# A gated cross-attention and mixture-of-experts layer: expert rows loaded two blocks at a time, and eight more zero products on TensorE at the head

## The chip, the cores and the metric

One core of a Trainium2 chip runs the whole layer in one launch. The metric is device time in microseconds; the kernel before was run three times for it, and one further execution was profiled. Engines are named as in the profile: PE is TensorE, DVE is VectorE, ACT is ScalarE, POOL is GpSimd, SP is the sync engine, which here does nothing but issue DMAs.

## The reference

4096 tokens (64 sequences of 64) of width 128, in float32:

```python
x = x + tanh(g_xattn[0]) * xattn(layernorm(x), ctx)
x = x + tanh(g_ffn[0]) * ffn(layernorm(x))

# xattn(Q, K): causal scores of K with itself, applied to Q
scores = einsum('btd,bsd->bts', K, K) * tril(ones)
return Q + einsum('bts,bsd->btd', scores, Q)

# ffn: one shared expert and the 2 best of 8 experts for each token
shared = silu(x @ shared_w1.T) @ shared_w2.T            # hidden width 512
top, idx = top_k(x @ gate_w.T, 2); gates = softmax(top)
selected = sum over the 2 experts of gate * (silu(x @ w1[e]) @ w2[e])
return shared + selected
```

## The kernel before

The tokens are 32 tiles of 128, in 8 groups of 4 tiles. The program of every engine is written out by hand, in order, with semaphores between them.

**Head (until about 74 us).** For each group PE makes the masked scores (`score`, L1099 and L1103), applies them (`apply_scores`, L1113), transposes the normalised rows n (`transpose_n`, L1120), makes logits in strips (`logit_strips`, L1128, and `logits`, L1134), and in between the shared expert's products (`shared_up`, L1164, and `shared_down`, L1177). ACT writes n tile by tile (L580), one semaphore count per tile, and `transpose_n` waits for each tile; ACT then copies the four transposed tiles out of the bank (L589) before the strips can be made. `keep_warm(times)` (L1184) issues products of a 128x128 with a 128x512 tile of zeros in bf16 into a bank that nobody reads; there are eight at the very start and five between `apply_scores(1)` and `transpose_n(0)`. DVE chooses the experts and the rows' places (`choose`, `place`); POOL then scatters the rows of n into a table in DRAM, sorted by expert, one indirect DMA per tile and choice (L516). The table's rows are 145 numbers (580 bytes): 128 of n and the routing data. The first 32 of these scatters are stage 0; SP waits for all of them before it loads any expert row.

**Expert blocks (from about 81 us).** The table is worked off in 71 blocks of 128 rows. Blocks 0 to 33 are full and come in 17 pairs: both blocks of a pair belong to one expert and lie next to each other in the table (the row of the second is that of the first plus 128). Blocks 34 to 70 stand alone. Blocks are loaded in sets of four (the first set has two): set 0 is blocks 0 and 1, set 1 is 2 to 5, set 2 is 6 to 9, set 3 is 10 to 13. `load_x(s)` on SP issues one DMA per block (L389) into a ring of 12 buffers, each with its own semaphore; ahead of each it reads the row's address into a register (L387, L388). `load_w1(i)` (L377 to L380) does the same for a 256 KB weight, one for each pair or single block, into a ring of 8.

The order on SP is: weights 0 and 1; wait for stage 0's scatters; sets 0 and 1; weights 2 and 3; set 2; weights 4 to 7; then, block by block, the next weight (its buffer is free when the up products of the pair 8 weights earlier are done, L379) and the set three further on. Weight 8 thus waits for the second up product, and set 3 stands behind it. Weight 9 also waits for DVE's second tables of addresses.

On PE `transpose_rows(s)` (L1289) waits for each block's semaphore and transposes it into one bank; DVE copies the bank to SBUF (`copy_xT`, L1007), and the next set's transposes wait for that copy. The order is set 0, the first up product (`up`, L1315), set 1, `counts`, the second up product, set 2, then for each block one up product and one down product (`down`, L1336), with set 3 ahead of the up product of block 6, set 4 ahead of that of block 10, and so on. ACT applies silu and the gate, POOL scatters each block's result to its tokens (L542), and after the last block SP and ACT load those rows back, DVE adds them, and the result is stored.

On DVE the copy of set 2 comes, in its queue, after the second tables (`tables_full`) and `region_ends`.

Of the kernel before, what the change touches and what calls it, by code (L numbers as in the profile page):

```python
# [5 lines left out]
def flamingo_gated_moe(nc, xP, ctxT, g_both, sw1T, sw2T, w1T, w2T, gateT, outP):  # L6
# [7 lines left out]
    ds = bass.ds  # L14

    P = 128
# [4 lines left out]
    E = w1T.shape[1] // H  # L21
# [4 lines left out]
    G = 4  # L26
# [23 lines left out]
    FULL = 2 * PAIRS  # L50
# [3 lines left out]
    SPARE = USED - K * TILES  # L54
    P_SHIFT = P.bit_length() - 1
    PADS = E + SPARE
    REGION = T + P
# [8 lines left out]
    SET = 4  # L66
    X_SETS = 3
# [7 lines left out]
    sets = [range(max(0, a), min(USED, a + SET)) for a in range(FULL % SET - SET, USED, SET)]  # L75
# [12 lines left out]

    def last_with(b):
        return b | 1 if b < FULL else b  # L90

    UP_BANKS, Y_BANKS = ((1, 2), (1, 2, 5, 6)), ((3, 7), (3, 7, 4))

# [13 lines left out]
    with stack:  # L107
        def sb(name, shape, dt=f32):
            return stack.enter_context(nc.sbuf_tensor(name, shape, dt))

        def sem(name):
            return stack.enter_context(nc.semaphore(name))

        x_dram = nc.dram_tensor("expert_rows", ((E + 1) * REGION, ROW), f32, kind="Internal").ap()
# [73 lines left out]
        row_at = sb("row_at", [1, USED], i32)  # L188
# [10 lines left out]
        x_ring = sb("x_ring", [P, X_RING, ROW])  # L199
# [71 lines left out]
        x_loaded = [sem(f"x_loaded{j}") for j in range(X_RING)]  # L271
# [16 lines left out]
        def at_least(eng, semaphore, value):  # L288
            if value > 0:
                eng.wait_ge(semaphore, value)  # L290
# [16 lines left out]
        def tile(g, t):  # L307
            return slice(g * GW + t * D, g * GW + (t + 1) * D)
# [28 lines left out]
        def _(sp):  # L337
# [27 lines left out]
            row_reg = [sp.alloc_register(f"sp_row{i}") for i in range(2)]  # L365
# [6 lines left out]
            def load_w1(i):  # L372
                slot_w = i % W_RING
                b = first_of(i)
                if b in (0, EARLY, FULL):
                    sp.wait_ge(tables_done, (0, EARLY, FULL).index(b) + 1)
                sp.reg_load(weight_reg[i % 2], weight_at[0:1, b:b + 1])  # L377
                at = sp.snap(weight_reg[i % 2], min_val=0, max_val=(E - 1) * H)
                at_least(sp, up_psum, last_with(first_of(i - W_RING)) + 1 if i >= W_RING else 0)  # L379
                sp.dma_start(w1_ring[:, slot_w], w1T[:, ds(at, H)]).then_inc(w1_in[slot_w], 16)  # L380

            def load_x(s):
                at_least(sp, xT_psum, s - X_SETS + 1)
                at_least(sp, gap_done, s - X_SETS + 1)
                for i, b in enumerate(sets[s]):
                    j = s % X_SETS * SET + i
                    sp.reg_load(row_reg[i % 2], row_at[0:1, b:b + 1])  # L387
                    at = sp.snap(row_reg[i % 2], min_val=0, max_val=E * REGION + (SPARE - 1) * P)  # L388
                    sp.dma_start(x_ring[:, j], x_dram[ds(at, P), :]).then_inc(x_loaded[j], 16)  # L389

            def y_complete(until):
                for j in range(Y_RING):
# [10 lines left out]
            load_w1(1)  # L403
            sp.wait_ge(x_scattered[0], 16 * STAGE_TILES[0])
            load_x(0)
            load_x(1)
            load_w1(2)
            load_w1(3)
            load_x(2)
            for i in range(4, W_RING):  # L410
                load_w1(i)
# [143 lines left out]
        def _(act):  # L555
# [151 lines left out]
            def silu(b):  # L707
                act.wait_ge(up_psum, b + 1)
                at_least(act, y_psum, last_with(b - H_SLOTS) + 1 if b >= H_SLOTS else 0)
                act.activation(hT[:, b % H_SLOTS], ps_up(b)[:, :], ACT.Silu).then_inc(hT_done, 1)  # L710
# [379 lines left out]
        def _(pe):  # L1090
# [16 lines left out]
            def apply_scores(g):  # L1107
                pe.wait_ge(scores_done, g + 1)
                at_least(pe, x1_done, g)
                for t in range(G):  # L1110
                    pe.wait_ge(q_done, G * g + t + 1)
                    cols = slice(t * P, (t + 1) * P)
                    last = pe.matmul(ps_q[:, cols], masked(g)[:, cols], q[:, g % 2, cols], start=True, stop=True)  # L1113
                last.then_inc(attn_psum, 1)

            def transpose_n(g):
                at_least(pe, strips_done, g)
                for t in range(G):
                    pe.wait_ge(n_done, G * g + t + 1)
                    last = pe.transpose(ps_n[:, t * P:(t + 1) * P], n[:, g * G + t, 0:D], ident[:, :])  # L1120
                last.then_inc(nT_psum, 1)

            def logit_strips(g):
                if g == 0:
                    pe.wait_ge(gT_in, 16)
                pe.wait_ge(nT_done, g + 1)
                for t in range(G):
                    last = pe.matmul(ps_strips[t * STRIP:(t + 1) * STRIP, :], gT[:, :], nT[:, tile(g, t)], start=True, stop=True)  # L1128
                last.then_inc(strips_psum, 1)
# [27 lines left out]
            def shared_up(i):  # L1157
                if i == 0:
                    pe.wait_ge(sw_in, 16)
                    pe.wait_ge(scores_done, 4)  # L1160
                pe.wait_ge(nT_done, i // HC + 1)
                at_least(pe, sT_done, i - 1)
                c = i % HC
                pe.matmul(ps_sup[i % 2][:, :], sw1[:, c * P:(c + 1) * P], nT[:, group(i // HC)],  # L1164
                          start=True, stop=True).then_inc(sup_psum, 1)
# [16 lines left out]
            def keep_warm(times):  # L1182
                for _ in range(times):
                    pe.matmul(ps_warm[:, :], warm[:, 0:P], warm[:, :], start=True, stop=True)  # L1184
# [6 lines left out]
            apply_scores(0)  # L1191
            score(3)
            apply_scores(1)
            keep_warm(5)
            transpose_n(0)
            logit_strips(0)
            shared_up(0)
            logits(0)
# [9 lines left out]
            shared_down(0, 0)  # L1208
            shared_down(0, 1)
            transpose_n(1)  # L1210
            apply_scores(3)
            shared_down(0, 2)
# [3 lines left out]
            shared_up(5)  # L1216
            shared_down(0, 3)
            transpose_n(2)
            shared_up(6)
            apply_scores(4)  # L1220
# [60 lines left out]
            def transpose_rows(s):  # L1281
                if s == 0:
                    pe.wait_ge(scores_done, GROUPS)
                at_least(pe, xT_done, s)
                for i, b in enumerate(sets[s]):
                    j = s % X_SETS * SET + i
                    earlier = sum(1 for r in range(s % X_SETS, s, X_SETS) if len(sets[r]) > i)
                    pe.wait_ge(x_loaded[j], 16 * (earlier + 1))
                    last = pe.transpose(ps_x[:, i * P:(i + 1) * P], x_ring[:, j, 0:D], ident[:, :])  # L1289
                last.then_inc(xT_psum, 1)  # L1290

# [34 lines left out]
            def down(b):  # L1326
                at = pe.snap(weight_reg[b % 4], min_val=0, max_val=(E - 1) * H)
                pe.wait_ge(hT_done, last_with(b) + 1)
                if earlier(b, Y_BANKS) >= 0:
                    pe.wait_ge(y_done, earlier(b, Y_BANKS) + 1)  # L1330
                elif bank_of(b, Y_BANKS) == 3:
                    pe.wait_ge(count_read, 1)
                else:
                    pe.wait_ge(shared_out, LATE)
                for c in range(HC):
                    last = pe.matmul(ps_y(b), hidden(b, c), w2[:, ds(at + c * D, D)],  # L1336
                                     start=(c == 0), stop=(c == HC - 1))
                last.then_inc(y_psum, 1)
# [7 lines left out]
            logits(7)  # L1346
            shared_up(27)
            transpose_rows(0)
            shared_down(5, 2)
            shared_down(5, 3)  # L1350
            positions(7)
            up(0)
            transpose_rows(1)
            counts()
            up(1)
            pe.wait_ge(w2_in, 32)
            for b in range(USED):
                if set_from.get(b + T_AHEAD, 0) > 1:
                    transpose_rows(set_from[b + T_AHEAD])
                if b + 2 == EARLY:  # L1360
                    pe.wait_ge(tables_done, 2)
                if b + 2 == FULL:
                    pe.wait_ge(tables_done, 3)
                if b + 2 < USED:
                    set_weights(b + 2)
                for a in range(b + up_ahead(b - 1), min(b + up_ahead(b) + 1, USED)):
                    up(a)
                down(b)
# [53 lines left out]
```

## Time and profile before

| | |
|---|---|
| median of 3 runs | 236.11 us (236.18, 236.11, 234.06) |
| profiled execution | 236.13 us, its span 234.3 us |
| PE busy | 225.7 us (96%) |
| POOL, ACT, DVE busy | 149.2 (64%), 133.1 (57%), 118.3 us (51%) |
| mean granted clock of TensorE | 0.993 |
| x_ring loads | 71 of 72.5 KB, 2.9 us to landing (median) |
| w_ring loads | 54 of 256 KB, 3.7 us to landing (median) |

The span runs from the first to the last instruction of the profiled execution; its time as the runs measure it is 1.8 us longer. A busy PE is not a PE at its peak: matmuls are pipelined and their ends modelled, so a row of four transposes that lasts 0.60 us is followed by the next work sooner than that. The granted clock is a share of 2.4 GHz.

### The profile page before, as it was taken

How to read it: one execution, taken by the hardware profiler on the slowest of the kernel's cores; microseconds unless marked ns; L12 is line 12 of the kernel's file. 1: busy time of each engine (PE TensorE's matmuls, PEld its weight loads, DVE VectorE, ACT ScalarE, POOL GpSimd, SP SyncE). 2: the span in 40 equal slices, each digit the busy share in tenths (PEclk: the TensorE clock that was granted, in tenths of full speed). 3: DMA queues.
4: the chain of work that ended last, by engine and by line, in shares of the span. 5: the costliest groups of instructions: out<-in, count | busy, mean ns of one | idle time of the engine just before them, and what ended most of it. 6: DMA issues, size and time to landing. Idle time of an engine off the chain costs nothing.

```text
span 234.3 us, 5945 instructions
## 1 busy us (share of the span) xinstructions
PE 225.7 (96%) x1669; PEld 196.3 (84%) x1671; DVE 118.3 (51%) x546; ACT 133.1 (57%) x303; POOL 149.2 (64%) x178
## 2 busy tenths in 40 slices
PE   7969999999999989899999999999999999999994
PEld 3926777767776769699999999999999999999884
DVE  6896796977776478498331222202221122268304
ACT  2654777678556645356555654565555655566520
POOL 4762574767777777787777777776445455565710
PEclk9997999999999999999999999999999999999999
DMA  6998011111116689666677426668876677699742
GB/s 239 267 425 327 29 50 32 51 51 54 63 52 159 139 230 282 175 180 181 178 188 190 154 79 207 209 206 253 248 220 208 209 229 228 205 315 405 267 150 90
DMA packets 30462, 43.46 MB, mean 186 GB/s; under 512 B 5232, under 2 KB 16752, under 8 KB 30176
## 3 DMA queue, kind: packets, MB, share of 16 engines
q1 hardware_dynamic: 25248, 32.87, 47.6%
q0 software_dynamic: 4320, 9.41, 11.0%
q10 hardware_dynamic: 864, 0.80, 1.0%
q8 instruction: 15, 0.25, 0.4%
q14 instruction: 15, 0.12, 0.2%
HBM read 30.45 MB, written 12.62 MB: 184 GB/s over the span
## 4 chain that ended last, share of the span: by engine, by line
PE 71%; POOL 8%; DMA 6%; SPq 6%; issue 5%; DVE 2%; ACT 1%; POOLq 1%; DVEq 0%
PE bank L1315 25%; PE bank L1336 24%; POOL expert_rows L516 6%; PE bank L1164 6%; PE bank L1177 4%; PE bank L1289 3%; PE bank L1103 3%; PE bank L1113 2%; DMA x_ring<-expert_rows 2%; SPq L389 2%; SPq L387 2%; PE bank L1184 2%; DMA nT<-y_rows 1%; DMA expert_rows<-n,slot 1%; SPq L380 1%
## 5 line engine op out<-in xcount | busy, mean ns | idle before, releaser
L542 POOL DMA_INDIRECT y_rows<-y,dest x71 | 71.4, 1006 | 39.0 <-ACT y L716 29.6
L516 POOL DMA_INDIRECT expert_rows<-n,slot x64 | 62.7, 980 | 28.5 <-issue 18.3
L1315 PE MATMUL bank<-xT,w_ring 128*128 128x128 f32 (+1 forms) x432 | 74.2, 309 | 0.4 <-issue 0.2
L1336 PE MATMUL bank<-w,hT 128*128 x568 | 74.5, 275 | 0.0
L1336 PEld LDWEIGHTS bank<-w,hT 128*128 128x128 f32 x568 | 71.3, 192 | 1.6
L710 ACT ACTIVATE hT<-bank 128x512 f32<-128x512 f32 x71 | 42.5, 598 | 37.9 <-PE bank L1315 37.8
L1315 PEld LDWEIGHTS bank<-xT,w_ring 128*128 128x128 f32 x432 | 59.3, 192 | 2.5 <-issue 0.7
L1007 DVE COPY xT<-bank 128x512 f32<-128x512 f32 (+2 forms) x19 | 12.4, 652 | 75.1 <-PE bank L1289 73.3
L716 ACT ACTIVATE y<-bank,gate 128x128 f32<-128x128 f32 x71 | 26.1, 368 | 21.2 <-PE bank L1336 20.8
L1177 PEld LDWEIGHTS bank<-sw,sT 128*128 128x128 f32 x224 | 27.4, 192 | 5.3 <-issue 5.0
L1164 PE MATMUL bank<-nT,sw 128*128 128x512 f32 x56 | 30.0, 633 | 0.0
L1177 PE MATMUL bank<-sw,sT 128*128 128x128 f32 x224 | 28.4, 276 | 0.0
L600 ACT ACTIVATE sT<-bank 128x512 f32<-128x512 f32 x28 | 16.4, 594 | 9.6 <-PE bank L1164 9.5
L570 ACT ACTIVATE q<-xres,shift,rstd 128x128 f32<-128x128 f32 x32 | 13.5, 488 | 4.8 <-POOL shift L478 3.4
L580 ACT ACTIVATE n<-xres,shift,rstd 128x128 f32<-128x128 f32 x32 | 13.7, 488 | 2.9 <-POOL shift L478 2.6
L748 DVE BATCH_NORM_STATS2 stats<-xres 128x6 f32<-128x128 f32 x64 | 13.9, 279 | 0.2
L1289 PE MATMUL bank<-ident,x_ring 128*128 128x128 f32 x71 | 12.1, 278 | 1.5 <-DMA x_ring<-expert_rows 1.4
L1164 PEld LDWEIGHTS bank<-nT,sw 128*128 128x128 f32 x56 | 9.2, 200 | 4.6 <-issue 4.6
L1289 PEld LDWEIGHTS bank<-ident,x_ring 128*128 128x128 f32 x71 | 8.6, 141 | 3.7 <-DMA x_ring<-expert_rows 1.9
L477 POOL TENSOR_TENSOR rstd<-var_eps,minus_half 128x4 f32<-128x4 f32 x8 | 8.2, 1024 | 4.2 <-DVE var_eps L757 4.1
L1103 PEld LDWEIGHTS bank<-kT 128*128 128x128 f32 x64 | 9.2, 207 | 1.1 <-issue 0.7
L1103 PE MATMUL bank<-kT 128*128 128x128 f32 x64 | 9.1, 288 | 0.1
(154 smaller groups left out, 199.9 us busy)
## 6 DMA issues: line engine op xcount, KB each, us to landing
w_ring<-in_w1T SPq DMA_DIRECT2D x54, 256.0 KB, 3.7
x_ring<-expert_rows SPq DMA_DIRECT2D x71, 72.5 KB, 2.9
w<-in_w2T SPq DMA_DIRECT2D x2, 1024.0 KB, 11.7
kT<-y_rows SPq DMA_DIRECT2D x8, 256.0 KB, 6.3
nT<-y_rows SPq DMA_DIRECT2D x7, 256.0 KB, 4.4
out<-xres SPq DMA_DIRECT2D x7, 256.0 KB, 4.8
kT<-in_ctxT SPq DMA_DIRECT2D x3, 512.0 KB, 7.0
xres<-in_xP SPq DMA_DIRECT2D x3, 512.0 KB, 7.7
```

The lines of the kernel that those rows point to most:

```text
L516: pool.indirect_dma_start(out=x_dram[:, :], out_offset=bass.IndirectOffsetOnAxis(ap=slot[:, i, k:k + 1], axis=0), in_=n[:, i, :], in_offse ...
L542: pool.indirect_dma_start(out=y_dram[:, :], out_offset=bass.IndirectOffsetOnAxis(ap=dest[:, b:b + 1], axis=0), in_=y[:, j], in_offset=None ...
L600: act.activation(sT[:, g % 2, i % HC], ps_sup[i % 2][:, :], ACT.Silu).then_inc(sT_done, 1)
L710: act.activation(hT[:, b % H_SLOTS], ps_up(b)[:, :], ACT.Silu).then_inc(hT_done, 1)
L716: act.activation(y[:, b % Y_RING], ps_y(b), ACT.Copy, scale=gate[:, b:b + 1]).then_inc(y_done, 1)
L748: dve.bn_stats(stats[:, which, g % 2, t, :], xres[:, tile(g, t)]).then_inc(part_done, 1)
L1103: last = pe.matmul(ps_s[g][:, t * P:(t + 1) * P], k_t, k_t, start=False, stop=(t == G - 1), skip_group_check=True)
L1164: pe.matmul(ps_sup[i % 2][:, :], sw1[:, c * P:(c + 1) * P], nT[:, group(i // HC)], start=True, stop=True).then_inc(sup_psum, 1)
L1177: last = pe.matmul(ps_so[g][:, cols], sT[:, g % 2, c, cols], sw2[:, c * D:(c + 1) * D], start=(c == 0), stop=(c == HC - 1))
L1289: last = pe.transpose(ps_x[:, i * P:(i + 1) * P], x_ring[:, j, 0:D], ident[:, :])
L1315: last = pe.matmul(ps_up(b)[:, j * width:(j + 1) * width], w1_ring[:, w % W_RING, c * P:(c + 1) * P], xT[:, s % X_SETS, i * P:i * P + widt ...
L1336: last = pe.matmul(ps_y(b), hidden(b, c), w2[:, ds(at + c * D, D)], start=(c == 0), stop=(c == HC - 1))
```

## The change

SP issues one DMA for both blocks of a pair: a block for which `leads` is true issues a DMA of two blocks (or of one, from block 34 on) into two neighbouring ring buffers, and counts on the first buffer's semaphore; the second block of a pair issues nothing. PE waits, for either block of a pair, on the first one's semaphore, and the number of loads that it waits for is counted from the sets that used this buffer as a leader. On PE `keep_warm` is called with 8 instead of 5 ahead of `transpose_n(0)`, with 1 behind each of the first three transposes of group 0, and with 2 behind all four: eight products more in all. Nothing else moves.

```diff
+    def leads(b):
+        return b >= FULL or b % 2 == 0
+
+    def leader(b):
+        return b if leads(b) else b - 1
...
                 for i, b in enumerate(sets[s]):
-                    j = s % X_SETS * SET + i
-                    sp.reg_load(row_reg[i % 2], row_at[0:1, b:b + 1])
-                    at = sp.snap(row_reg[i % 2], min_val=0, max_val=E * REGION + (SPARE - 1) * P)
-                    sp.dma_start(x_ring[:, j], x_dram[ds(at, P), :]).then_inc(x_loaded[j], 16)
+                    if leads(b):
+                        j = s % X_SETS * SET + i
+                        blocks = last_with(b) + 1 - b
+                        reg = row_reg[i // blocks % 2]
+                        sp.reg_load(reg, row_at[0:1, b:b + 1])
+                        at = sp.snap(reg, min_val=0, max_val=E * REGION + (SPARE - 1) * P)
+                        sp.dma_start(x_ring[:, j:j + blocks, :], x_dram[ds(at, blocks * P), :].rearrange("(i p) d -> p i d", p=P))\
+                            .then_inc(x_loaded[j], 16)
...
                     last = pe.transpose(ps_n[:, t * P:(t + 1) * P], n[:, g * G + t, 0:D], ident[:, :])
+                    if g == 0 and t < G - 1:
+                        keep_warm(1)
                 last.then_inc(nT_psum, 1)
...
             apply_scores(1)
-            keep_warm(5)
+            keep_warm(8)
             transpose_n(0)
+            keep_warm(2)
             logit_strips(0)
...
                     j = s % X_SETS * SET + i
-                    earlier = sum(1 for r in range(s % X_SETS, s, X_SETS) if len(sets[r]) > i)
-                    pe.wait_ge(x_loaded[j], 16 * (earlier + 1))
+                    first_i = i - (b - leader(b))
+                    loads = sum(1 for r in range(s % X_SETS, s + 1, X_SETS) if len(sets[r]) > first_i and leads(sets[r][first_i]))
+                    pe.wait_ge(x_loaded[s % X_SETS * SET + first_i], 16 * loads)
```

## Rows read from the trace of the kernel before

**Rows 1.** The page's chain that ended last: shares of the span by engine.

```profile
PE 71%; POOL 8%; DMA 6%; SPq 6%; issue 5%; DVE 2%; ACT 1%; POOLq 1%; DVEq 0%
```

**Rows 2.** Stretch 20 to 72 us: length, then each engine's busy time, clock, DMA share, GB/s.

```profile
20.00:72.00 52.00, 51.94 (x360) 38.69 (x360) 39.94 (x235) 36.89 (x84) 33.67 (x36) 1.00 0.22 66
```

**Rows 3.** Stretches around the clock's fall: PE, PEld, DVE, ACT, POOL, clock, DMA, GB/s.

```profile
13.00:16.50 3.50, 1.34 (x5) 0.55 (x4) 3.36 (x20) 2.36 (x6) 2.92 (x6) 1.00 1.04 422
16.00:21.00 5.00, 4.46 (x17) 2.09 (x18) 4.42 (x33) 2.80 (x7) 2.16 (x7) 0.66 1.00 416
```

**Rows 4.** Timeline of PE at the head: start, duration, instructions [idle before them].

```profile
12.00 1.03 PE L1184 MATMUL bank<-warm 128*128 128x512 bf16 x4
14.27 1.48 PE L1120 MATMUL bank<-ident,n 128*128 128x128 f32 x4 [1.25 <-ACT n L580]
16.54 0.63 PE L1128 MATMUL bank<-nT,gT 128*32 128x128 f32 x8 [0.78 <-ACT nT L589]
17.09 2.07 PE L1164 MATMUL bank<-nT,sw 128*128 128x512 f32 x2
...
23.57 1.02 PE L1164 MATMUL bank<-nT,sw 128*128 128x512 f32 x2
```

**Rows 5.** The chain of waits in order of time: start, duration, what.

```profile
51.65 0.23 DVE slot L853
...
74.42 0.27 SPq L387
...
98.16 0.89 PE bank L1336 x8
99.05 0.87 PE bank L1315 x4
```

**Rows 6.** Timeline of SP's DMA issues: first start, first start to last end.

```profile
74.87 4.57 SPq L389 DMA_DIRECT2D x_ring<-expert_rows  x6
...
81.62 3.02 SPq L389 DMA_DIRECT2D x_ring<-expert_rows  x4
85.18 4.18 SPq L380 DMA_DIRECT2D w_ring<-in_w1T  x5
89.93 2.80 SPq L389 DMA_DIRECT2D x_ring<-expert_rows  x4
```

**Rows 7.** Timeline of PE from 80 to 98 us.

```profile
80.84 0.38 PE L1289 MATMUL bank<-ident,x_ring 128*128 128x128 f32 x2
...
83.89 0.60 PE L1289 MATMUL bank<-ident,x_ring 128*128 128x128 f32 x4
...
84.36 1.11 PE L1315 MATMUL bank<-xT,w_ring 128*128 128x256 f32 x4
...
87.18 0.33 PE L1289 MATMUL bank<-ident,x_ring 128*128 128x128 f32 x1 [0.45 <-DMA x_ring<-expert_rows]
87.65 1.10 PE L1315 MATMUL bank<-xT,w_ring 128*128 128x256 f32 x4
...
93.86 1.05 PE L1336 MATMUL bank<-w,hT 128*128 x8
95.44 0.30 PE L1289 MATMUL bank<-ident,x_ring 128*128 128x128 f32 x1 [0.53 <-DMA x_ring<-expert_rows]
...
97.06 1.10 PE L1315 MATMUL bank<-xT,w_ring 128*128 128x256 f32 x4 [0.23 <-issue]
```

**Rows 8.** Stretches with scatters alone, with x loads, with weights: columns as above.

```profile
64.00:68.00 4.00, 4.00 (x28) 2.38 (x27) 3.42 (x20) 2.36 (x6) 3.09 (x4) 1.00 0.19 58
78.00:80.00 2.00, 2.00 (x20) 1.15 (x19) 0.50 (x3) 1.16 (x3) 1.52 (x2) 1.00 0.62 145
90.00:92.00 2.00, 2.00 (x15) 1.87 (x14) 1.76 (x10) 1.18 (x5) 1.41 (x2) 1.00 0.93 311
```

**Rows 9.** The tile x_ring from 74 to 100 us: issue to landing.

```profile
DMA to landing us min/median/max: 2.0/2.9/4.1
```

**Rows 10.** Timeline of DVE from 91 to 93 us.

```profile
91.87 0.67 DVE L1007 COPY xT<-bank 128x512 f32<-128x512 f32 x1
```

## The prediction

> **What bounds the kernel now.** I read the chain that ended last first, then stretches of the span, then each engine's order of work where the chain leaves TensorE (PE). PE holds 71% of the chain [rows 1], and from 20 to 72 us it is busy 51.94 of 52 us [rows 2]: there only less or faster PE work counts. The reader is to look for the places where PE is slow or idle *and* on the chain. There are two.
>
> The first is the clock at the head. From 16 to 21 us the mean granted clock is 0.66, that is, the lower level (1.2 GHz) for about two thirds of it; before, in 13 to 16.5 us, the row shows PE busy 1.34 of 3.5 us at the full 2.4 GHz, and then the clock falls [rows 3]. PE had stood idle 1.25 us before the first transposes of n, took them one by one as ScalarE delivered, and idled 0.78 us again before the logits' strips [rows 4]. Then it works without a gap, so slow time is lost time: two 512-column products take 2.07 us at 17.09, and 1.02 us at 23.57 [rows 4].
>
> The second is between 84 and 97 us, where the first expert rows arrive. The sync queue (SP) issues one x load about every 0.85 us ((4.57 - 0.33) / 5 in the first six) [rows 6]. PE's sets 0 and 1 are transposed without waiting (80.84, 83.89), but set 2 comes in piece by piece until 87.18, and set 3 from 95.44 on [rows 7]; the waits named are for x loads. After 97.06 PE shows no wait for a load any more, so what is won before that point goes to the end. Whatever of SP's work is saved later is worth nothing: PE's dense work of the expert blocks hides it.
>
> **The change part by part.**
>
> *Three products more ahead of the first transposes, three among them, two behind.* A zero product takes at most 1.03 / 4 = 0.26 us [rows 4]. The three ahead (0.78) lie inside the 1.25 us of idle time. Among the transposes, one transpose each 0.38 us is what ScalarE allows ((1.48 - 0.33) / 3) [rows 4]; four of them back to back take 0.47 at most (83.89 to 84.36) [rows 7], so 0.12 each, and 0.12 + 0.26 = 0.38 just fits. What does not fit is changing the weights of the array in between, of which no row shows how much is hidden: from 0 to 0.2 us per product, so 0 to 0.6 us on the chain to the first logits. I take 0.15, since the sum without it fits. The two behind (0.52) lie in the 0.78 us in which PE waits for ScalarE's copy; if that cover were gone they would cost 0.52. Cost: 0.15.
>
> *What they give.* The fall costs 5 x (1 - 0.66) = 1.70 us of full-speed work [rows 3]. Does it go away? With the products PE does some 8 x 0.26 = 2.1 us more between 12.9 and 16.5 us, and no idle time longer than about 0.5 us is left there. The trace has two stretches thinner than that in which the clock did not move: 84.36 to 87.65 holds about 0.87 + 0.47 us of work, and from the end of the row at 93.86 to 97.06 there are four transposes [rows 7]. So I take the whole 1.70; the ends are 0 and 1.70. Net 1.55.
>
> Does it reach the end? PE, VectorE and ScalarE hang on each other there, and PE has no slack to lose until 72 us [rows 2]. The 1.55 us go through the slots of the third group (51.65) into GpSimd's uninterrupted run of scatters, whose last first-stage transfer releases SP at 74.42 [rows 5]. If GpSimd took only part of it, sets 0 and 1 have cover (set 0 could land by 77.3, used at 80.84), and set 2 would give back about 0.6 us: that is the lower bound of this step.
>
> *Paired loads.* Of the x loads that SP issues before set 3 is complete, 14 become 7. An issue stays at about 0.33 us plus its register work (no row here shows a two-block x load; ends: 0.33, and twice that if it grew with its rows; I take 0.33, and even 0.33 more on each of the seven would be 2.3 us, the rival below). New times, with 74.87 as start and 0.85 a step: set 0 is issue 1, set 1 issues 2 and 3, weights 4 and 5, set 2 issues 6 and 7 at 79.1 and 80.0 (before from 81.62 on), four weights to 83.4 (before from 85.18). The next weight waits, as it always did, for the second up product to end: 84.36 + 0.87 = 85.2 [rows 5, 7]; before, that was long over, now SP stands there about 1 us, and set 3 behind it. Set 3 goes out at 86.2 and 87.1 instead of 89.93 to 92.4 [rows 6].
>
> Do the DMA engines follow? While only x loads run they are busy 0.62, scatters alone make 0.19 [rows 8], so one block costs (0.62 - 0.19) x 0.85 = 0.37 us of the engines; with weights 0.93 at 311 GB/s, less 0.19 and 58, a 262 KB weight costs 0.74 x 262 / 253 = 0.77 us. Ahead of set 3's end: 14 x 0.37 + 7 x 0.77 = 10.6 us; at the 0.74 that the scatters leave of the highest row, 14.3 us from 75.2 on, so 89.5, and 1.6 us of completion (the shortest landing, 2.0 [rows 9], less 0.37): 91.1. Set 2, in the same way (10 blocks, 2 weights: 5.2 us / 0.74), lands at 83.9, before PE is free at 85.2. At an engine share of 0.75 instead of 0.93 set 3 would land at about 95.7.
>
> What PE then does: set 2 is transposed at 85.23 to 85.70 and the third up product starts there and not at 87.65: 1.95 us. The blocks after it move with it; their last down product, which starts at 93.86 and takes 0.89 [rows 5, 7], ends at 92.80. Set 3 (0.47) to 93.27, then the up product that started at 97.06: 3.79 us in all. Late next is VectorE: its copy of set 2 must be over before set 3 may go into the same bank. That copy stands in its own queue behind the second tables and ends at 91.87 + 0.67 = 92.54 [rows 10], 0.26 us before PE comes. It is the new neighbour of the bound, and the reason why an even earlier set 3 gains nothing. The next load of SP that waits for those second tables, and set 4 behind it, is needed only some 7 us later.
>
> One place where a rule and the rows differ: at this pace the issue of an x load (0.85 us) is longer than its engine time (0.37 us) [rows 6, 8]. The Trainium skill, "DMA: Bandwidth & Descriptors", section "Issuing engines are not separate DMA queues", says that saving a sequencer's issue time is usually small beside the transfer itself. By it set 2's wait would go and set 3's would be set by the engines, as in the first rival.
>
> **Sum.** 1.70 - 0.15 + 3.79 = 5.34 us; of it I give 0.2 back for the paired issue and the 0.26 us margin: 5.1. The profiled execution took 236.13 us (span 234.3), 0.02 above the median of 236.11: 236.13 - 5.1 = **231.0 us**, span 229.2. One of the three runs before stands at 234.06, 2.1 us below the others, about what a head without the clock's fall would give.
>
> **Rivals.**
> - *The DMA engines set set 3* (15%). For: 0.93 busy around 91 us. Against: 0.62 before it, room for the work to move up. Landing at 95.7 instead of 91.1 gives back 2.9 us: 233.9; at a share of 0.80, about 94.2 and 232.4.
> - *The clock falls all the same, or falls in a neighbouring stretch* (13%). For: no row shows how much work is enough. Against: the two thinner stretches. 236.13 + 0.15 + 0.2 - 3.79 = 232.7. The Trainium skill, "TensorE: Matmul & The Clock Gate", "What's actually happening", says that the moment of a change varies from run to run; the 234.06 run agrees.
> - *The gain is taken back by another engine* (9%): the head's 1.55 us stop at GpSimd or VectorE, or VectorE's copy comes 2 us late; 234 to 235.
> - *The two-block transfer costs the DMA engines more than two single ones* (5%). Place: the wait of set 3. At 0.74 us of the engines a pair lands at 91.1. It ends slower than before if set 3 lands 1.55 us after the old 96.5, so 6.9 us later: 6.9 x 0.74 / 7 = 0.73 more per pair, double. At three times, 13.9 us later, 243. For: no row shows one. Against: the same rows of the same length over the same queue.
> - *It does nothing measurable* (3%): fewer issues, but each as long as the two it replaces; then SP's times stay and, with no head gain, 236.
>
> **Numbers.** My forecast has 55%, with 230.0 to 232.0 as its own range (clock gain 1 to 1.7, waits 3.2 to 3.79, and the runs' own scatter). The range reaches over the second rival and most of the first: 229.7 to 233.6. About 1% (2.4 us) is what a measurement of this kernel can tell from no change. Faster by more: the forecast, the clock rival and nearly all of the DMA one, 0.84; within 1%: the third and the last, 0.11; slower: 0.05.
>
> **What would show it.** Clock 1.00 from 16 to 21 us and two 512-column products of shared_up in about 1.0 us there; 54 x loads instead of 71, the set-3 pair issued about 3.5 us sooner against 74.42's counterpart; no wait of PE on x_ring above 0.2 us; the up product that stands 22.2 us after the first x issue now (97.06 - 74.87) 18.4 us after it. Wrong would be: a wait left at set 3 (first rival), the clock still at 0.5 (second), an x landing much above 4 us (fourth), or a PE gap named VectorE.

## The result, and the profile after

The changed kernel takes 232.62 us (median of 4 executions, 232.36 to 232.85), the kernel before 236.15 us beside it (4 executions, 234.06 to 236.79): a ratio of 0.9898 [0.9852, 0.9945], so 1.0% faster where 2.2% was forecast. By the medians it is 3.53 us, or 1.5%. The ratios here and below leave out disturbed executions, so they need not equal the quotient of two medians. The profiled execution of the changed kernel took 232.85 us (span 231.0), 3.28 us less than the one before.

First the page: the chain that ended last by engine, the granted clock in 40 slices, and the x loads (size, median us to landing).

```profile
PE 91%; DMA 2%; POOL 2%; DVE 1%; issue 1%; SPq 1%; ACT 1%; DVEq 0%
...
PEclk9999999999999999999999999999999999999999
...
x_ring<-expert_rows SPq DMA_DIRECT2D x37, 72.5 KB, 2.1
x_ring<-expert_rows SPq DMA_DIRECT2D x17, 145.0 KB, 3.9
```

PE holds 91% of the chain instead of 71% [rows 1], the clock shows no dip, and 54 x loads are left of 71. Yet DMA and POOL still stand on the chain with 2% each. Where?

The head, as stretches (length, then PE, PEld, DVE, ACT, POOL busy, clock, DMA share, GB/s).

```profile
13.00:16.50 3.50, 2.55 (x19) 0.91 (x17) 3.40 (x20) 2.61 (x7) 2.92 (x7) 1.00 1.05 425
16.00:21.00 5.00, 4.72 (x33) 3.40 (x34) 4.72 (x35) 3.52 (x10) 1.90 (x7) 1.00 1.00 418
```

From 16 to 21 us the clock is 1.00, where it was 0.66 [rows 3]; PE is busy 2.55 us ahead of it instead of 1.34. PE's timeline shows how the products sit there (start, duration, what [idle before]):

```profile
11.53 1.89 PE L1196 MATMUL bank<-warm 128*128 128x512 bf16 x8
14.02 0.33 PE L1130 MATMUL bank<-ident,n 128*128 128x128 f32 x1 [0.60 <-ACT n L590]
14.18 0.38 PE L1196 MATMUL bank<-warm 128*128 128x512 bf16 x1
14.40 0.33 PE L1130 MATMUL bank<-ident,n 128*128 128x128 f32 x1
...
15.33 0.59 PE L1196 MATMUL bank<-warm 128*128 128x512 bf16 x2
16.27 0.43 PE L1140 MATMUL bank<-nT,gT 128*32 128x128 f32 x8 [0.35 <-ACT nT L599]
16.63 1.13 PE L1176 MATMUL bank<-nT,sw 128*128 128x512 f32 x2
```

The transposes start 0.38 us apart, as before, with a product in each gap. From the first transpose to the strips it is 2.25 us (16.27 - 14.02), against 2.27 [rows 4]: the products cost nothing on the chain. Two 512-column products now take 1.13 us instead of 2.07.

Now SP's x loads (first start, first start to last end), set by set: sets 0 and 1; 2; 3; and, at 134.87, set 9.

```profile
73.35 2.21 SPq L398 DMA_DIRECT2D x_ring<-expert_rows  x3
...
77.76 1.25 SPq L398 DMA_DIRECT2D x_ring<-expert_rows  x2
79.50 4.60 SPq L386 DMA_DIRECT2D w_ring<-in_w1T  x5
85.18 1.30 SPq L398 DMA_DIRECT2D x_ring<-expert_rows  x2
...
134.87 2.83 SPq L398 DMA_DIRECT2D x_ring<-expert_rows  x4
```

And PE at the same sets: set 0; sets 2 and 3, each with the up product behind it; set 9 with its own.

```profile
78.94 0.38 PE L1303 MATMUL bank<-ident,x_ring 128*128 128x128 f32 x2
...
83.46 0.63 PE L1303 MATMUL bank<-ident,x_ring 128*128 128x128 f32 x4
83.96 1.10 PE L1329 MATMUL bank<-xT,w_ring 128*128 128x256 f32 x4
...
91.06 0.60 PE L1303 MATMUL bank<-ident,x_ring 128*128 128x128 f32 x4
91.50 1.03 PE L1329 MATMUL bank<-xT,w_ring 128*128 128x256 f32 x4
...
136.82 0.30 PE L1303 MATMUL bank<-ident,x_ring 128*128 128x128 f32 x1
137.57 0.33 PE L1303 MATMUL bank<-ident,x_ring 128*128 128x128 f32 x1 [0.45 <-DMA x_ring<-expert_rows]
138.40 0.33 PE L1303 MATMUL bank<-ident,x_ring 128*128 128x128 f32 x1 [0.50 <-DMA x_ring<-expert_rows]
139.25 0.33 PE L1303 MATMUL bank<-ident,x_ring 128*128 128x128 f32 x1 [0.52 <-DMA x_ring<-expert_rows]
139.72 1.10 PE L1329 MATMUL bank<-xT,w_ring 128*128 128x256 f32 x4
```

Sets 2 and 3 come without a wait, and the up product behind set 3 starts at 91.50 instead of 97.06 [rows 7]: 5.56 us are won there. But at set 9 there is a wait that the trace before does not have. There PE passed in one piece:

```profile
142.34 0.60 PE L1289 MATMUL bank<-ident,x_ring 128*128 128x128 f32 x4
142.77 1.03 PE L1315 MATMUL bank<-xT,w_ring 128*128 128x256 f32 x4
```

The up product behind set 9 moved from 142.77 to 139.72, by 3.05 us. So 2.51 of the 5.56 us are given back at this one place, and the end, 3.3 us earlier by the spans, follows from there.

Who holds set 9? It is the first set of single blocks (34 to 37), whose rows include those that POOL scatters for the tokens' second choice. SP waits for the last of these scatters. SP's waits from 98 to 150 us after (us in total, times, longest):

```profile
SPq L296 <- DMA expert_rows<-n,slot: 10.5, 1, 10.5
```

and before:

```profile
SPq L290 <- DMA expert_rows<-n,slot: 7.8, 1, 7.8
```

SP comes earlier and waits longer. POOL issues these last 16 x scatters one for one with the scatters of results (y). After:

```profile
129.50 0.96 POOL L526 DMA_INDIRECT expert_rows<-n,slot  x1 [0.30 <-issue]
130.77 0.96 POOL L552 DMA_INDIRECT y_rows<-y,dest  x1 [0.31 <-issue]
132.03 0.96 POOL L526 DMA_INDIRECT expert_rows<-n,slot  x1 [0.30 <-issue]
```

The last of these is the last x scatter of all. Before, it stood here:

```profile
134.01 0.96 POOL L516 DMA_INDIRECT expert_rows<-n,slot  x1 [0.30 <-issue]
```

So POOL moved by 1.98 us, which is nearly the head's gain (its uninterrupted run begins at 50.24 instead of 52.15), and not by the pairs'. An x scatter every 2.53 us is its own pace. The chain of waits of the changed kernel runs through exactly this:

```profile
132.03 2.31 DMA expert_rows<-n,slot
...
134.87 0.33 SPq L398
...
137.37 1.83 DMA x_ring<-expert_rows
...
139.25 0.33 PE bank L1303
```

Before, set 9's loads went out here:

```profile
137.79 2.77 SPq L389 DMA_DIRECT2D x_ring<-expert_rows  x4
```

The last of the four was issued at 140.23 (137.79 + 2.77 - 0.33), and the four loads took 1.8 us each to land by this trace, so set 9 was in at about 142.0, 0.3 us ahead of PE's 142.34. Set 9 had hardly any slack, and no wait showed it.

POOL's 1.98 us are not all of the 3.05. Before, SP issued set 9 at 137.79, 3.78 us after the start of the last x scatter; after, 2.84 us after it (134.87 - 132.03). The trace's records of landings show why. SP's wait counts 16 increments for a scatter, and before, 15 of them had come by 136.32 and the last at 137.28; after, all 16 were in by 134.35. So some 0.9 us of the profiled difference come from one late part of one transfer in the execution before, which no part of the change moved. That is luck. Without it set 9 would have had about 1.2 us of slack before (an estimate: 0.3 + 0.9).

### The profile page after: what moved, and what is told of

Read it like the earlier page. It is cut to its first block, busy times and chain, and to the rows that moved or that the text cites. A ratio compares the mean times of both kernels' runs of the same rounds, so it can differ in the third digit from the quotient of the medians.

```text
span 231.0 us, 5895 instructions
## 1 busy us (share of the span) xinstructions
PE 224.4 (97%) x1679; PEld 195.6 (85%) x1679; DVE 118.0 (51%) x546; ACT 132.9 (58%) x303; POOL 147.8 (64%) x178
## 4 chain that ended last, share of the span: by engine, by line
PE 91%; DMA 2%; POOL 2%; DVE 1%; issue 1%; SPq 1%; ACT 1%; DVEq 0%
PE bank L1350 26%; PE bank L1329 25%; PE bank L1176 11%; PE bank L1189 11%; PE bank L1303 3%; PE bank L1123 3%; PE bank L1113 3%; PE bank L1196 2%; PE bank L1130 2%; PE bank L1397 2%; PE bank L1386 1%; PE bank L1140 1%; DMA expert_rows<-n,slot 1%; POOL y_rows L552 1%; DMA x_ring<-expert_rows 1%
## 5 line engine op out<-in xcount | busy, mean ns | idle before, releaser
L552 POOL DMA_INDIRECT y_rows<-y,dest x71 | 69.1, 974 | 39.0 <-ACT y L726 28.9
L526 POOL DMA_INDIRECT expert_rows<-n,slot x64 | 63.6, 993 | 26.9 <-issue 18.3
L1176 PE MATMUL bank<-nT,sw 128*128 128x512 f32 x56 | 28.6, 608 | 0.0
L1303 PE MATMUL bank<-ident,x_ring 128*128 128x128 f32 x71 | 11.6, 276 | 1.5 <-DMA x_ring<-expert_rows 1.5
L1176 PEld LDWEIGHTS bank<-nT,sw 128*128 128x128 f32 x56 | 8.7, 190 | 4.1 <-issue 4.1
L1113 PEld LDWEIGHTS bank<-kT 128*128 128x128 f32 x64 | 8.7, 197 | 1.0 <-issue 0.7
L1113 PE MATMUL bank<-kT 128*128 128x128 f32 x64 | 8.6, 277 | 0.0
## 6 DMA issues: line engine op xcount, KB each, us to landing
x_ring<-expert_rows SPq DMA_DIRECT2D x37, 72.5 KB, 2.1
```

Of the source, the lines that this page charges most:

```text
L526: pool.indirect_dma_start(out=x_dram[:, :], out_offset=bass.IndirectOffsetOnAxis(ap=slot[:, i, k:k + 1], axis=0), in_=n[:, i, :], in_offse ...
L552: pool.indirect_dma_start(out=y_dram[:, :], out_offset=bass.IndirectOffsetOnAxis(ap=dest[:, b:b + 1], axis=0), in_=y[:, j], in_offset=None ...
L1113: last = pe.matmul(ps_s[g][:, t * P:(t + 1) * P], k_t, k_t, start=False, stop=(t == G - 1), skip_group_check=True)
```

## Experiments

Theory A: what PE wins beyond POOL's own 1.98 us and the little slack of set 9 is lost there, because POOL's second-choice scatters release it. Theory B: the two parts add up to their sizes at sets 0 to 3, and the loss is elsewhere. All kernels below are edits of the kernel before or of the changed one. "Clock kept" counts the executions with a mean granted clock of 0.997 or more; one fall at the head gives about 0.993, and two about 0.985. Each ratio is to the kernel before on the same chip: the first four experiments ran on one chip, the other eight on another.

| kernel | median us (executions) | ratio to before | clock kept |
|---|---|---|---|
| **pairs_only** | 235.52 (12) | 0.999 [0.9951, 1.0029] | 1 of 12 |
| **products_only** | 234.15 (12) | 0.9927 [0.9898, 0.9955] | 10 of 12 |
| **both_scatters_early** | 231.32 (6) | 0.9828 [0.9786, 0.9871] | 6 of 6 |
| **pairs_scatters_early** | 233.26 (6) | 0.9892 [0.9838, 0.9946] | 1 of 6 |
| **after_again** | 233.35 (12) | 0.9947 [0.9909, 0.9985] | 9 of 12 |
| **both_addresses_ready** | 233.01 (7) | 0.9896 [0.9862, 0.9931] | 7 of 7 |
| **eight_ahead_only** | 234.84 (12) | 0.994 [0.9898, 0.9981] | 5 of 12 |
| **among_behind_only** | 233.78 (12) | 0.9958 [0.9918, 0.9999] | 8 of 12 |
| **products_scatters_early** | 233.82 (12) | 0.9967 [0.9936, 0.9998] | 12 of 12 |
| **both_scatters_early_2** | 231.23 (6) | 0.9852 [0.9804, 0.99] | 6 of 6 |
| **both_ring_only** | 235.16 (12) | 1.0018 [0.9977, 1.0058] | 4 of 12 |
| **both_order_only** | 230.58 (6) | 0.9824 [0.9776, 0.9872] | 6 of 6 |

The kernel before, in its executions beside these: clock kept in 2 of 23 on the first chip and in 19 of 53 on the second (8 of 30 beside the four kernels from after_again on, 11 of 23 beside the last four); 21 of 76 in all.

### Each part alone

**pairs_only**: the changed kernel with the head of before.

```
-                    if g == 0 and t < G - 1:
-                        keep_warm(1)
...
-            keep_warm(8)
+            keep_warm(5)
             transpose_n(0)
-            keep_warm(2)
```

> Paired loads with the old head (five products ahead of the first transposes, none after). Theory A (set 9 is held by GpSimd's second-choice scatters of the late groups, which no part of the paired loads moves): PE reaches 97 us work 3.5 to 3.9 us earlier, then waits 2.5 to 3.5 us for x_ring at set 9 (near 137 to 142 us), and the kernel gains 0.2 to 1.3 us over before: 234.9 to 235.9. Rival B (the two parts simply add and something of the head was lost): the full 3.8 us, 232.3, no wait at set 9.

Its trace at sets 2 and 3 is as forecast (up products at 86.30 and 93.90, no wait), and then PE stands at set 9:

```profile
139.34 0.30 PE L1300 MATMUL bank<-ident,x_ring 128*128 128x128 f32 x1
140.22 0.33 PE L1300 MATMUL bank<-ident,x_ring 128*128 128x128 f32 x1 [0.58 <-DMA x_ring<-expert_rows]
...
142.21 1.10 PE L1326 MATMUL bank<-xT,w_ring 128*128 128x256 f32 x4
```

Set 3's up product stood 3.16 us earlier than before (97.06 - 93.90), that of set 9 only 0.56 (142.77 - 142.21), and the time is that of before. POOL's last x scatter has not come earlier (134.01 before):

```profile
134.49 0.96 POOL L526 DMA_INDIRECT expert_rows<-n,slot  x1 [0.31 <-issue]
```

A holds: without a gain of POOL's, that of the pairs is nearly gone by set 9. The 0.56 us that are left come from the slack, since here the last scatter released SP 2.3 us after its start.

**products_only**: the eight products, with the single loads of before (the diff above the other way round, on the kernel before).

> The eight zero products with the old single loads. A: the clock stays at 1.00 from 16 to 21 us, PE and GpSimd both move by 1.7 to 2.0 us, the waits at sets 2 and 3 stay, set 9 comes just in time as before: 234.1 to 234.5, that is, more than half of the 3.5 us that both parts gave. B (the head's gain is lost on the way): within 0.5 us of before.

The waits at sets 2 and 3 are there as before, and set 9 passes at once:

```profile
140.23 0.60 PE L1292 MATMUL bank<-ident,x_ring 128*128 128x128 f32 x4
```

POOL and PE have moved together, by 2.24 (134.01 to 131.77) and 2.11 us (142.34 - 140.23). That is A. So the time that the change gives is nearly all the products'.

### The scatters that hold set 9, earlier

**both_scatters_early**: POOL issues two of the 16 second-choice scatters behind each of the first eight y scatters, instead of one behind each of the first 16. Results then wait longer for their scatter, so the ring of y buffers is made longer.

```
-                if b < len(later):
-                    g, t = later[b]
-                    scatter_x(g, t, 1)
+                for g, t in later[2 * b:2 * b + 2]:
+                    scatter_x(g, t, 1)
...
-    Y_RING = 12
+    Y_RING = 16
```

> The changed kernel with GpSimd's 16 second-choice scatters two behind each of the first eight y scatters instead of one behind each of sixteen, and a y ring of 16 buffers instead of 12 so that the y scatters may come later. A: the scatters end near 121 us instead of 133, set 9 is in time, PE shows no wait on x_ring after 90 us: 2.3 to 2.8 us off 232.6, so 229.8 to 230.3. B: set 9's wait is the engines' or the loads' own, and the time stays at 232.3 to 232.8.

SP issues set 9 ten microseconds earlier (in after at 134.87):

```profile
124.78 2.76 SPq L398 DMA_DIRECT2D x_ring<-expert_rows  x4
```

and PE takes it in one piece:

```profile
137.05 0.60 PE L1302 MATMUL bank<-ident,x_ring 128*128 128x128 f32 x4
```

The wait is gone and the kernel is the faster, as A has it; but 231.32 is 1 us above what was expected. In this profile the end was not PE's: the chain ended with the last y scatter, the load of those rows and DVE's additions.

```profile
217.39 2.22 DMA y_rows<-y,dest
...
220.69 3.31 DMA nT<-y_rows
...
224.70 0.43 DVE xres L1065
```

**pairs_scatters_early**: the same two edits on pairs_only.

> Paired loads with the old head, and the scatters moved forward as in the kernel with both parts. A: now the paired loads give what sets 2 and 3 cost, 3.5 to 3.9 us: 232.2 to 232.7. B: like the paired loads alone.

No wait on an x load is left (set 9 at 139.12, four transposes at once), and it is 2.3 us below pairs_only (235.52 - 233.26), of the 3.16 won at set 3. The time is 0.6 us above the range expected, but B, by which the early scatters give nothing, is out.

**products_scatters_early**: the same two edits on products_only, as a counter-test: where PE does not wait at set 9, early scatters should be worth nothing.

> The eight products with single loads, and GpSimd's second-choice scatters moved forward with the y ring of 16. A (set 9 is late only for a PE that the paired loads brought there sooner): with single loads set 9 came just in time, so at most 0.3 us off the 234.15 of the products alone, 233.8 to 234.4. B (the early scatters are a gain of their own, by themselves): 1.3 us or more, below 232.9.

233.82, beside 233.49 for those executions of the kernel before on this chip that kept their clock: nothing. The early scatters pay only together with the pairs.

**both_scatters_early_2**: both_scatters_early once more, on the second chip.

> The fastest kernel once more, beside the others of this group on one chip: 231.0 to 231.6, clock 0.997 or more.

231.23, as on the first.

### Which of the two edits

**both_ring_only**: the changed kernel with the longer y ring and the old order.

> The changed kernel with the y ring of 16 and the old order of the scatters. A: no gain, 232.6 to 233.4, the wait at set 9 as in the changed kernel. B (the y ring held something): 0.5 us or more faster.

Set 9 waits as in after (0.52, 0.42 and 0.44 us), so the ring gives nothing. That it came out at 235.16 was not expected: the clock was kept in 4 of 12 executions (median 233.64) and fell in the rest, with the same head as in after. Why it fell oftener here is open.

**both_order_only**: the changed kernel with the early scatters, and the ring left at 12.

> The changed kernel with the scatters moved forward and the y ring left at 12. A: the wait at set 9 goes, but the y scatters now come so late (the ninth is complete near 125 us) that ACT cannot write the 21st y block near 122.5 us: 2 to 3 us of wait there, passed on to PE by the y banks; 231.8 to 233.5, no gain or a loss against the changed kernel. B (the ring has room): as with the ring of 16, 231.3.

My own expectation, that the short ring would bind, was wrong. ACT does wait for a y buffer (us in total, times, longest):

```profile
ACT y L725 <- DMA y_rows<-y,dest: 3.4, 2, 2.6
```

but PE passes set 9 without a wait (137.13) and the chain ends on PE's last shared products:

```profile
222.40 3.59 PE bank L1396 x32
```

In the changed kernel the same row reads:

```profile
224.62 3.59 PE bank L1397 x32
```

2.22 us earlier, the span 2.2 us shorter. At 230.58 us, 0.9824 [0.9776, 0.9872], it is the fastest kernel here, 0.65 us ahead of both_scatters_early_2 on the same chip; why the longer ring costs that is open. The time lies in the range that was forecast for the change alone, but beside a kernel before that keeps its clock in 11 of 23 executions here.

### Another way at the same wait

**after_again**: the changed kernel, on the second chip, as the measure for the next three.

> The changed kernel once more, beside the kernels of this group on the same chip. Both theories: 232.3 to 232.9; it is the measure for the other three.

233.35, a little above: in 3 of 12 executions the clock fell (median 235.07), in the other nine it is 233.23. The kernel before, where it kept its clock on this chip and in the same comparison (8 of 30), has a median of 233.39. With the clock kept in both, the change is worth 0.2 us here (in the first comparison 1.4, but against the single execution at 234.06).

**both_addresses_ready**: SP reads set 9's four row addresses into registers while it waits for the scatters, and then issues the four loads one behind the other (`set9_addresses` holds the four register loads, `load_set9` the four DMAs, both as in `load_x`).

```
+                        ats = set9_addresses()
                         sp.wait_ge(padded_out, 16 * (E + 1))
                         sp.wait_ge(x_scattered[2], 16 * STAGE_TILES[2])
-                    load_x(set_from[b] + X_SETS)
+                        load_set9(ats)
```

> The changed kernel; SP reads the four row addresses of set 9 into registers ahead of its waits and not between the loads, so the four loads follow each other by about 0.45 us and not 0.85. A (the loss at set 9 is the late release plus SP's pace of single loads: the first block was there 0.1 us after PE, the fourth 2.5 us after): the fourth issue comes about 1.2 us sooner and the kernel gains 1.0 to 1.2 us. B (the loss is the release alone, or the transfers themselves): within 0.3 us of the changed kernel.

The four issues take less time (in after 2.83):

```profile
135.42 1.91 SPq L403 DMA_DIRECT2D x_ring<-expert_rows  x4
```

and from the start of the last x scatter to the up product behind set 9 it is 6.68 us (132.87 to 139.55), 1.08 less than in after_again (132.22 to 139.98), as A has it. But the kernel's time is only 0.2 us below that of after_again with its clock kept (233.01 and 233.23), which is what B expected. The profile is of the slowest of the seven executions (233.73), and in it the head stood 0.65 us later (set 0 at 79.58, against 78.93); whether the edit causes that stays open. For the size it is inconclusive.

### Which of the products

**eight_ahead_only**: eight ahead of the transposes, none among or behind them. **among_behind_only**: five ahead as before, with the three among and two behind.

> The changed kernel without the five products among and behind the transposes: eight ahead, none after. A (it is the idle time between and behind the transposes that let the clock fall): the clock falls in most executions, mean granted clock 0.985 to 0.993, 1.5 to 2.5 us slower than the changed kernel, near the paired loads with the old head (235.5). B (the idle time ahead of the transposes was the cause): as the changed kernel, clock 0.998 or more.

> The changed kernel with five products ahead as before, and the five among and behind the transposes kept. A: the clock stays in most executions, within 0.5 us of the changed kernel. B: the clock falls as before, 1.5 to 2.5 us slower than the changed kernel.

The clock was kept in 5 of 12 and 8 of 12 executions, against 8 of 30 of the kernel before and 9 of 12 with all eight in the same comparison. With the clock kept they take 232.99 and 233.22, like after_again; where it fell once, 235.01 and 234.94. So the three ahead by themselves can hardly be told from before, the five among and behind do more, and what they change is how often the clock stays up, not the time of an execution in which it does. With groups of 12 that order is not settled: both_ring_only has all eight and kept it in 4 of 12, and the kernel before in 11 of 23 in the later comparison. All eight against none is clearer: over every kernel here with all eight (the first four executions of the changed kernel included) the clock was kept in 64 of 77 executions, over every one with the old head in 23 of 94 (the four executions of the kernel before in the first section are not among them).

## Why the prediction went wrong, step by step

- **The head.** Right. The three products fit into ScalarE's gaps at 0.38 us a step and cost nothing (0.15 was taken). PE's set 0 came 1.90 us earlier and POOL's run 1.91; the first transpose itself was 0.25 us earlier, for which the change gives no reason, and that leaves 1.65 for the clock, against a forecast of 1.55.
- **It reaches sets 0 to 3.** Right: SP was released early enough that the first x load went out 1.52 us sooner (74.87 to 73.35).
- **The issue of a pair.** Right. Two pairs took 1.30 us, so 0.97 from one to the next, hardly more than 0.85 for a single block. The up product behind set 3 stood 18.15 us after the first x issue (18.4 forecast). The Trainium skill, "DMA: Bandwidth & Descriptors", section "Issuing engines are not separate DMA queues", calls a sequencer's issue time usually small beside the transfer; here an issue, at a step of 0.85 us, is shorter than the 1.8 us that a block of set 9 takes to land, and yet it set the pace: the waits at sets 2 and 3 went when the issues were halved with the same bytes, and set 9's four singles came at the pace of their issues. At set 3 the issues were not all: before, 15 of the 16 increments of its last block had come by 94.83, and the last at 96.45, by the trace's records of landings.
- **The DMA engines and VectorE.** Right, by a small margin: the engines' share was 1.04 from 84 to 86 us and 0.38 from 88 to 90, but the second pair of set 3, issued at 86.10, took 4.7 us to land, so it was in at 90.8, 0.3 us before PE came at 91.06. With the head's 1.52 us taken off, the forecast's 91.1 would have been 89.6. An x landing much above 4 us was named as a sign of the fourth rival; it came, and cost nothing here. DVE's copy of set 2 ended at 90.70 (90.03 + 0.67), 0.36 us before PE (0.26 forecast).
- **The failed step: "After 97.06 PE shows no wait for a load any more, so what is won before that point goes to the end."** The first half is what the trace before shows; the second doesn't follow. A stage later on, set 9, was released by POOL and came in 0.3 us ahead of PE. POOL's pace has nothing to do with PE's x loads, so only the 1.98 us by which POOL itself moved, set 9's slack and the 0.9 us of the late part before could pass. The next sentence of the prediction, that whatever of SP's work is saved later is worth nothing, fails with it: both_order_only gains by an earlier set 9. At set 9 there was 5.56 us of gain and 3.05 left; with the 0.25 us that the spans show behind it, that is 3.3 instead of the 5.1 forecast. Of this the paired loads' 3.79 were hit: alone they give 0.999 [0.9951, 1.0029].
- **The rival that came nearest** was the gain taken back by another engine; it named GpSimd, but for the head's 1.55 us, and not for the pairs'. It gave 234 to 235; the changed kernel lies between it and the forecast. By its number alone the clock rival (232.7) was nearest to the measured 232.62, but that is luck, since the clock stayed at 1.00. "No wait of PE on x_ring above 0.2 us" was the sign to look for, and it showed the fault at once: 0.45, 0.50 and 0.52 us at set 9.
- **The base.** The sum was made against one execution with a fallen clock, 0.02 us above the median. The median is a mixture: the kernel before keeps its clock in 21 of 76 executions, with medians of 233.4 to 234.1, against 235.3 to 235.5 with one fall. The 234.06 run was read rightly as such a run, but its meaning for the price was not drawn: the products' gain is in how many executions keep the clock, and a median moves with that. With the clock kept in both kernels the change is worth 0.2 us (after_again), so nearly all that the medians show is the clock. The Trainium skill, "TensorE: Matmul & The Clock Gate", section "What's actually happening", says that the point of the change varies from run to run. The runs here show something beside it: whether a fall comes at all varies, with none in 21 of 76 executions of one program.

## What to carry to other kernels

A trace without a wait doesn't show slack. Before a gain is carried to the end, go through every later stage that waits on another engine's semaphore, take how long before its use it came in, and ask whether what paces it moves too. If not, the gain ends there, and the remedy is in that engine's order of work: here two scatters behind each of eight y scatters instead of one behind each of 16, worth 2.65 us on top of the paired loads (after_again with its clock kept, 233.23, to both_order_only, 230.58) where the paired loads by themselves gave none. And slack read from one execution can hold luck: here 0.9 us of it were one late part of one transfer. And where the clock falls in some executions and not in others, count them over many before a median is explained.

## What the runs showed of the hardware

- The same program kept TensorE's clock in some executions and lost it in others, and the share differed by chip (2 of 23 and 19 of 53 for the kernel before). One fall cost about 2 us on the second chip (233.39 to 235.37, and 233.49 to 235.34).
- Loads of 72.5 KB landed in 2.1 us and those of 145 KB in 3.9 (medians, from different stretches of the changed kernel), and yet sets 2 and 3 came in sooner as pairs; one issue to the next took SP 0.97 us for a pair and 0.85 for a single block.
- POOL started its scatters of 128 rows 1.26 to 1.27 us apart, x and y alike (129.50, 130.77, 132.03), and 2.31 us after the start of the last one SP was released. In the kernel before that took 3.3 us, because one of the 16 increments came 0.96 us behind the others (137.28 and 136.32).
